# The last layer's selective scan: one scan, one read product and one GpSimd product for each state, over all three channel groups, with the decays in SBUF

## The reference

```python
# xc, sz: (32 images, 50 tokens, 384 channels);  B, C: (32, 50, 16 states)
delta = softplus(dt @ w_dt + b_dt)                       # 384 channels
A     = -exp(A_log)                                      # 384 x 16
h     = 0
for t in range(50):                                      # along the tokens of an image
    h = exp(delta[t] * A) * h + (delta[t] * xc[t]) * B[t]   # 384 x 16
    y[t] = sum over states of h * C[t]  +  D_skip * xc[t]
out = (y * sz) @ w_out
```

## Time and profile before

| | us |
|---|---|
| median of three runs | 2648.09 (2644.2 to 2649.54) |
| the profiled execution, its own time | 2642.21 |
| its span, first to last instruction | 2640.4 |
| TensorE busy in the span | 2083.9 (79%) |
| Vector engine | 1244.3 (47%) |
| ScalarE | 887.3 (34%) |
| GpSimd | 758.3 (29%) |

### The profile page before, as it was taken

One profiled execution on the slowest core, in us unless ns is written; L12 is line 12 of the kernel. 1 busy time (PEld: TensorE's weight loads), 2 busy tenths in 40 slices (PEclk: granted clock), 3 DMA queues, 4 the chain that ended last, 5 costly groups with the idle time before them and its releaser, 6 DMA issues. The chain is left out here.

```text
span 2640.4 us, 41973 instructions
## 1 busy us (share of the span) xinstructions
PE 2083.9 (79%) x13260; PEld 1499.9 (57%) x13260; DVE 1244.3 (47%) x2879; ACT 887.3 (34%) x1789; POOL 758.3 (29%) x700
## 2 busy tenths in 40 slices
PE   9746778887975885886898847777399935999998
PEld 9412225675754773663566312224289825999987
DVE  4349993334643114644013789998422245222222
ACT  1247873223332332442213645553122212212111
POOL 0104541003112552000001156774134311444443
PEclk9758996786966995987999879999599956999999
DMA  7000000000005760000220000000367615777774
GB/s 215 20 0 1 0 0 1 0 0 7 0 0 156 208 156 27 0 0 0 72 71 0 0 1 0 0 0 0 108 191 227 171 41 164 219 225 222 226 202 125
DMA packets 77951, 201.86 MB, mean 76 GB/s; under 512 B 17777, under 2 KB 47348, under 8 KB 69524
## 3 DMA queue, kind: packets, MB, share of 16 engines
q1 hardware_dynamic: 52820, 169.74, 20.1%
q0 software_dynamic: 25056, 31.22, 6.8%
HBM read 179.25 MB, written 22.91 MB: 77 GB/s over the span
## 5 line engine op out<-in xcount | busy, mean ns | idle before, releaser
L1865 POOL DMA_INDIRECT sums<-yblock,put x129 | 205.8, 1596 | 420.6 <-DVE yblock L2128 247.9
L1913 PE MATMUL banks<-xTblock,wt 128*128 128x256 f32 (+1 forms) x1464 | 268.0, 340 | 1.6 <-ACT xTblock L1984 1.2
L2118 DVE TENSOR_TENSOR hid<-sa,banks 128x512 f32<-128x512 f32 (+1 forms) x183 | 105.7, 578 | 339.4 <-ACT sa L2005 336.5
L1938 PE MATMUL banks<-wt,hid 128*128 128x192 f32 x1548 | 265.6, 326 | 0.0
L2005 ACT ACTIVATE sa<-banks 128x512 f32<-128x512 f32 (+1 forms) x183 | 93.3, 510 | 481.2 <-PE banks L1924 476.2
L1913 PEld LDWEIGHTS banks<-xTblock,wt 128*128 128x128 f32 x1464 | 237.1, 194 | 23.4 <-issue 1.6
L1938 PEld LDWEIGHTS banks<-wt,hid 128*128 128x128 f32 x1548 | 249.8, 190 | 0.2
L738 PE MATMUL banks<-g,consts 128*128 128x400 f32 x384 | 184.7, 572 | 60.1 <-DVE g L877 56.2
L846 POOL TENSOR_TENSOR w<-u,spreadB 128x400 f32<-128x400 f32 x192 | 192.8, 1035 | 87.1 <-ACT spreadB L817 87.1
L1860 POOL DMA_INDIRECT xblock<-table,take x135 | 135.1, 1000 | 228.7 <-DVE put L2094 180.4
L871 DVE TENSOR_TENSOR_SCAN s<-banks,w 128x400 f32<-128x400 f32 x192 | 187.5, 977 | 4.2 <-POOL w L846 4.2
(11 more groups left out here) (420 smaller groups left out, 3730.9 us busy)
## 6 DMA issues: line engine op xcount, KB each, us to landing
wt<-L3f_packed SPq DMA_DIRECT2D x41, 1152.0 KB, 5.8
wt<-L3f_packed SPq DMA_DIRECT2D x41, 576.0 KB, 6.0
wt<-L3m_packed SPq DMA_DIRECT2D x20, 1152.0 KB, 5.8
wt<-L_packed SPq DMA_DIRECT2D x20, 579.0 KB, 4.4
wt<-L3m_packed SPq DMA_DIRECT2D x20, 577.0 KB, 6.0
wt<-L_packed SPq DMA_DIRECT2D x20, 576.0 KB, 3.9
pixels<-pixels SPq DMA_DIRECT2D x16, 375.0 KB, 4.2
wu<-L_up SPq DMA_DIRECT2D x8, 576.0 KB, 4.6
```

The costliest lines, as they stand in the source:

```text
L1865: nc.gpsimd.indirect_dma_start(t.sums, bass.IndirectOffsetOnAxis(put[:, q:q + 1], 0), y[:, b % 2, q - column_of_block[b], :], None, comput ...
L1913: nc.tensor.matmul(bank[:, n * j:n * (j + 1)], wt[:, v, cols(base, 2 * p + j)], xT[:, v, 0, 0:n], start=(j == 0), stop=False, skip_group_c ...
L1938: last = nc.tensor.matmul(bankY[s], hid[:, m, 128 * s:128 * (s + 1)], wt[:, v, DOWN_AT + DIM * m:DOWN_AT + DIM * (m + 1)], start=(m == 0 a ...
L2118: nc.vector.tensor_tensor(hid[:, 2 * p:2 * p + 2, 0:n], sa[:, (PAIRS * v + p) % 2, 0:2 * n].rearrange("p (m n) -> p m n", m=2), second[:, ...
```

## The change

`scan` is written for the last layer alone (layer 0 has a scan function of its own, which stays), and a job is now a state of all three groups:

- the decays lie in SBUF, in `behind`, as two slots of 128 x 3 x 400; ScalarE still writes them with three exponentials for a state, but signals once; one memset of 2400 columns clears both slots at the start.
- one GpSimd product of 128 x 1200 a state: `u` of the three groups times `spreadB`, repeated over the groups by a stride of 0.
- one scan of 128 x 1200 a state, the three groups one behind the other in one line; the zeros at the first token of each image also cut between the groups.
- one read product of 128 x 1200 a state, with the spread C row in PSUM repeated by a stride of 0.
- `w2`, `s` and `g` have two slots of a state each (before: four of a job). GpSimd's product of state n waits for the scan of state n - 2.
- the B rows get two PSUM banks instead of one, since the decays no longer need any; at the start of a chunk TensorE spreads two B rows and two C rows ahead.
- the order on the Vector engine is scan of state n, read of state n - 1; the additions on TensorE are three in a row for a state.

The core of the diff:

```diff
-        w2, s, g_ = (t.sbuf(n, [parts, SLOTS, CHUNK], st) for n in ("w2", "s", "g"))
-            bankA, bankB, bankC, acc = (t.bank[1], t.bank[7]), t.bank[0:1], t.bank[2:4], t.bank[4:7]
-        decays = [b[0:parts, 0:CHUNK] for b in bankA]
+        decays = spare[:, 0:2 * groups * CHUNK].rearrange("p (v g n) -> p v g n", v=2, g=groups)
+        w2, s, g_ = (t.sbuf(n, [parts, 2, groups, CHUNK], st) for n in ("w2", "s", "g"))
+        bankB, bankC, acc = t.bank[0:2], t.bank[2:4], t.bank[4:4 + groups]
+        line = lambda x, v: x[:, v].rearrange("p g n -> p (g n)")
...
+                    def spread_c(n):
+                        pe.wait_ge(g_done, c * STATES + n + 1)
+                        spread_row(bankC[n % 2], STATES + n).then_inc(spread, 1)
...
+                    spread_b(0)
+                    spread_b(1)
+                    spread_c(0)
+                    spread_c(1)
+                    for n in range(STATES):
+                        if n + 2 < STATES:
+                            spread_b(n + 2)
+                        sum_states(n)
+                        if n + 2 < STATES:
+                            spread_c(n + 2)
...
+                    def decay(n):
+                        act.wait_ge(s_done, c * STATES + n + 1)
+                        for g in range(groups):
+                            last = nc.scalar.activation(decays[:, n % 2, g, :].rearrange("p (b t) -> p b t", t=SEQ)[:, :, 1:SEQ],
+                                                        rate[:, g, at].rearrange("p (b t) -> p b t", t=SEQ)[:, :, 1:SEQ],
+                                                        ACT.Exp, scale=coef[:, g, n:n + 1])
+                        last.then_inc(a_done, 1)
...
-                            pool.wait_ge(s_done, c * jobs + j + 1)
-                            pool.wait_ge(b_copied, c * STATES + n + 3)
-                            nc.gpsimd.tensor_tensor(w2[:, j % SLOTS, :], u[:, g, at], spreadB[:, n % 2, :],
-                                                    ALU.mult).then_inc(bu_done, 1)
+                        pool.wait_ge(s_done, c * STATES + n + 1)
+                        pool.wait_ge(b_copied, c * STATES + n + 3)
+                        nc.gpsimd.tensor_tensor(w2[:, n % 2], u[:, :, at], spreadB[:, n % 2, :].unsqueeze(1).to_broadcast([parts, groups, CHUNK]),
+                                                ALU.mult).then_inc(bu_done, 1)
...
-                nc.vector.memset(decays[0], 0.0)
-                nc.vector.memset(decays[1], 0.0).then_inc(a_zero, 1)
+                nc.vector.memset(decays[:], 0.0).then_inc(a_zero, 1)
...
-                        nc.vector.tensor_tensor_scan(s[:, j % SLOTS, :], decays[j % DECAYS],
-                                                     w2[:, j % SLOTS, :], 0.0, ALU.mult, ALU.add).then_inc(s_done, 1)
+                        nc.vector.tensor_tensor_scan(line(s, n % 2), line(decays, n % 2), line(w2, n % 2), 0.0, ALU.mult, ALU.add).then_inc(s_done, 1)
...
-                        nc.vector.tensor_tensor(g_[:, j % SLOTS, :], s[:, j % SLOTS, :],
-                                                bankC[(j // groups) % 2][0:parts, 0:CHUNK], ALU.mult).then_inc(g_done, 1)
+                        nc.vector.tensor_tensor(g_[:, n % 2], s[:, n % 2], bankC[n % 2][0:parts, 0:CHUNK].unsqueeze(1).to_broadcast([parts, groups, CHUNK]),
+                                                ALU.mult).then_inc(g_done, 1)
...
-        scan(t, u, rate, coef, bc, xc, w["L3_D"], xc, bilinear=False)
+        scan(t, u, rate, coef, bc, xc, w["L3_D"], xc, flat(behind[:]))
```

More of the change, by code:

```diff
@@ L673, in _, with scan @@
                     last.then_inc(y_done, 1)
-def scan(t, u, rate, coef, bc, direct, gain, y, bilinear):
+def scan(t, u, rate, coef, bc, direct, gain, y, spare):
     nc = t.nc
@@ L769, in _ @@
                 act.wait_ge(a_zero, 1)
[L770 to L773, removed]
+                act.sem_inc(b_copied, 2)
                 nc.scalar.preload_act_table_set("natural_log_exp_and_others")
@@ L791, in decay @@
[L791 to L823, removed]
+                    def copy_b(n):
+                        act.wait_ge(b_spread, c * STATES + n + 1)
+                        act.wait_ge(bu_done, c * STATES + n + 1)
+                        nc.scalar.activation(spreadB[:, n % 2, :], bankB[n % 2][0:parts, 0:CHUNK], ACT.Identity).then_inc(b_copied, 1)
@@ L825, in _ @@
+                    copy_b(0)
+                    for n in range(STATES):
+                        if n + 1 < STATES:
+                            copy_b(n + 1)
+                        decay(n)
             @block.gpsimd
             def _(pool):
[L827 to L842, removed]
-                            pool.wait_ge(s_done, c * jobs + j + 1)
-                            pool.wait_ge(b_copied, c * STATES + n + 3)
-                            pool.sem_inc(t.passed, 1)
-                            nc.gpsimd.tensor_tensor(w2[:, j % SLOTS, :], u[:, g, at], spreadB[:, n % 2, :],
-                                                    ALU.mult).then_inc(bu_done, 1)
@@ new lines, in _ @@
+                pool.sem_inc(bu_done, 2)
+                with pool.Fori(0, CHUNKS) as c:
+                    at = bass.ds(CHUNK * c, CHUNK)
+                    for n in range(STATES):
+                        pool.wait_ge(s_done, c * STATES + n + 1)
+                        pool.wait_ge(b_copied, c * STATES + n + 3)
+                        pool.sem_inc(t.passed, 1)
+                        nc.gpsimd.tensor_tensor(w2[:, n % 2], u[:, :, at], spreadB[:, n % 2, :].unsqueeze(1).to_broadcast([parts, groups, CHUNK]),
+                                                ALU.mult).then_inc(bu_done, 1)
@@ L874, in read @@
-                    def read(j):
-                        dve.wait_ge(s_done, c * jobs + j + 1 + SLOTS)
-                        dve.wait_ge(spread, c * STATES + j // groups + 1)
-                        nc.vector.tensor_tensor(g_[:, j % SLOTS, :], s[:, j % SLOTS, :],
-                                                bankC[(j // groups) % 2][0:parts, 0:CHUNK], ALU.mult).then_inc(g_done, 1)
[L880 to L883, removed]
-                        if not bilinear:
-                            recur(j)
-                        if j:
-                            read(j - 1)
-                        if bilinear:
-                            recur(j)
@@ L893, in _ @@
+                    for n in range(STATES):
+                        recur(n)
+                        if n:
+                            read(n - 1)
+                    read(STATES - 1)
+                    dve.wait_ge(summed, c * STATES + STATES + 2)
                     for g in range(groups):
```

83 lines of the change are left out of this document (24 added, 59 removed).

## The result

| | before | changed |
|---|---|---|
| median, us | 2648.4 (2644.2 to 2649.5) | 3082.6 (3080.2 to 3086.1) |
| ratio, 95% interval | | 1.164 (1.162 to 1.166) |
| span of the profiled execution, us | 2640.4 | 3081.2 |

The sign was forecast, the size was not: 434 us more instead of 101. The difference lies in the scan stage. From its first GpSimd product (1552.21) to the start of its last final addition (2262.3) it now takes 710 us instead of 276.

What follows compares the result with a forecast made beforehand. The Vector engine sets the pace of the last layer's scan; 91.6 us for scan and product excluding each other, 1.6 clearing and 7.8 clock make 101.0 on 2642.2, plus 5.9 to the median: 2749 us, range 2718 to 2780.

Steps and rivals of the forecast that it cites:

- the exclusion: Last layer's scan stage: scan and GpSimd product hold each other off, 5.25 us a state, 91.6 us more; 85 in 100.
- ScalarE costs nothing: Last layer's scan: three exponentials and one copy, 2.3 us a state, hidden behind scan and product, adding nothing.
- S and P: Per state of the last layer's scan: S the merged scan, 2.65 us; P the merged GpSimd product, 2.71 us.
- the clock part: TensorE's clock in the scan stage: nothing in steady state, 15.6 us at the ends of four chunks, half taken, 7.8.
- the lower one: TensorE's lower clock level in the scan stage: 4.73 us a state, hidden under the 5.25 us period.
- No exclusion: Last layer's scan does not take part in the wait with GpSimd's product: 2648 to 2653 us; 9 in 100.
- The two share: Last layer's scan and GpSimd product partly overlap: half the extra period, 39 us, remains, 2692 us in all; 6 in 100.
- TensorE becomes the bound: Scan stage at the lower clock: 4.73 us a state exceed 3.95, not 5.25; matters only with No exclusion; no own chance.

Runs made afterwards that it cites:

- Stretching the ring over two states: Changed kernel, ScalarE's decays issued ahead of the next B row's copy: 2787.0 us; or, separately, TensorE's B row spread one state earlier: 2766.6 us.
- both swaps: Changed kernel with ScalarE's decays issued ahead of the next B row's copy and TensorE's B row spread one state earlier: 2766.2 us.
- removing the exclusion inside the ring: Changed kernel in its own order, the scan reading constant decays from PSUM instead of SBUF: 2989.9 us.
- the kernel that shows it: Kernel with both swaps, the scan reading constant decays from PSUM instead of SBUF: 2660.8 us, 1.004 of the kernel before.

## Why the prediction was wrong

**What bounds the kernel, and the exclusion: right.** The Vector engine set the pace. Moving the decays to SBUF made scan and product exclude each other, as the rows ahead of the scan had shown with other operations; a scan is now shown to take part (4.09 us against 2.66 in the two kernels that differ in that operand). The Trainium skill, "SBUF — State Buffer", section "Who interferes with whom", has such a wait last for the whole instruction of the other engine; the stands of 1.2 to 1.4 us behind products in mid-run agree in kind. But scan and product of 400 columns pass each other every 1.68 us where their records add up to 2.01, so the records are an upper bound of what excludes.

**The step that failed: "ScalarE costs nothing: ... started when the scan two states back ends and hidden behind S and P", and with it the clock part's "in the steady state the lower one costs nothing".** Both compare an engine's busy time with the period, as if its work could slide under the scan. I followed the semaphores of each instruction (the decay waits for the scan two states back, line by line correct), but not what stands in front of it in its engine's queue: the copy of B row n + 2, and by it TensorE's additions of state n - 1. The ring's own sum would have given the result. The prediction's figures, put end to end along it, are 2.3 us for decays and copy, 3.9 for the scan with its wait, 1.35 for the read, 3.90 for additions at the lower clock and 0.4 for one spread: 11.9 us a state, not 5.25. In the timeline above the shorter turn has 2.12 us from copy to scan, 3.74 to the read, 1.43 to the additions and 4.25 to the next copy, together 11.54; the mean of the turns is 11.97. Stretching the ring over two states, in either of two places, brings the kernel to 2766 to 2787 us, within 1.4% of the 2749 that were forecast. With both swaps the time lies in the forecast range, though not quite by its mechanism: a state takes 5.80 us there on average and not 5.25, and the ring over three states has a part in it.

**Why the same order was harmless before.** The kernel before has the same succession: the spread of B row n + 2 stands behind the additions of state n - 1, and its copy ahead of the last decay of state n + 1. But there the last read of state n - 1 comes five jobs ahead of the scan that this decay serves, five times 1.36 us, 6.8 us for the way by TensorE and ScalarE. With a state as the job the read stands directly ahead of that scan, and nothing is left of the 6.8 us. That the merging did this is argued from the two orders; that the order is what costs was shown by the swaps.

**The clock: mis-sized.** It was priced at 0 in the steady state and 15.6 us at most; filling the pauses in 48 of 64 states gives back 98 us. The price follows from the failed step: in a ring the additions' duration counts in full.

**The parts do not add up.** Stretching the ring takes off 316 us, removing the exclusion inside the ring 93, filling the pauses 98. Together that is more than 434, because the parts share the same chain, and a stand or a slow addition costs only while the ring binds. What is left after the swaps, 118 us, is what the exclusion does there (105, its stands inside the ring of three among them); the last 13 lie outside the steady state.

**The rivals.** "No exclusion" was priced at 2648 to 2653 us; the kernel that shows it needs 2661. "The two share" is out: a product that starts 0.24 us after a scan takes 2.2 us longer, nearly all that was left of the scan. "TensorE becomes the bound" was seen only as throughput; as a member of a ring it cost far more than its busy time says. A rival that the prediction does not have is the number of slots, two states in place of four jobs. It was not tested by itself; the kernel with the decays in PSUM keeps the two slots and runs at 4.09 us a state, so without the exclusion they cost nothing in the steady state. No version found here beats the kernel before: with no stand left and the ring no longer binding, the merged scan runs at its very pace.

## What to carry to other kernels

Before a wait is costed at nothing, walk the ring: for each instruction ask not only which semaphore it waits for but what stands ahead of it in its engine's queue, and follow that across engines until you come back to where you started; the period is at least the sum along the ring, its stands included, divided by the states it spans. Merging small jobs into big ones keeps the order on paper and takes away the distance in it: look ahead by one more step on each engine in the same edit, or check that a prefetch does not stand behind work of the step it is to run ahead of. And when an operand moves from PSUM to SBUF, count the SBUF inputs of the Vector engine's instruction and look who runs on GpSimd at that time. The count is not the whole test: the tensor_scalar at 1497.82 has one tensor operand and stood behind GpSimd's product too, 2.88 us instead of 0.48.

## What the runs showed of the hardware

- A scan with two SBUF inputs and a GpSimd product of two SBUF tensors exclude each other, whoever comes second: scans of 4.09 instead of 2.66 us, products of 4.95 instead of 2.75.
- The 1200-column scan takes 2.66 us with its decays in PSUM and 2.66 us with both inputs in SBUF when no product runs (the scan at 1719.56 of the changed kernel):

```profile
1719.56 2.66 DVE L811 TENSOR_TENSOR_SCAN s<-plain,w 128x1200 f32<-128x1200 f32 x1
```

The Trainium skill, "VectorE: DVE Perf Modes", section on the errata, gives a PSUM source a fixed part of 120 cycles and an SBUF source 58, 62 fewer; with one operand of two moved, these rows show no difference.
- Work that nobody reads can make a kernel faster: 40 idle matrix products a state brought the additions behind them from 4.37 or 3.87 to 2.28 us and the granted clock (1560 to 1700 us) from 0.63 to 0.94. Half as many, with a pause of 3.74 us behind them, brought the additions nothing.
